# Second attention of a four-layer gated model: turned value products, with divisors spread by TensorE

## Chip, cores and metric

One NeuronCore of a Trainium2 chip. The metric is device time of one execution in microseconds (us); lower is better. TensorE is called PE, VectorE DVE, ScalarE ACT, GpSimd POOL, as in the profile.

## The reference, cut to what matters

The model takes x (2 batches of 1024 rows, 256 wide) through four gated layers, each a cross attention and a feed-forward part. The change touches only the second layer's attention:

```python
def _L1_xattn_ref(query, key, value, attention_bias, Wq, Wk, Wv, Wo):   # 16 heads of 16
    q = proj(query, Wq, SQ); k = proj(key, Wk, SKV); v = proj(value, Wv, SKV)
    scores = jnp.einsum('bhqd,bhkd->bhqk', q, k) / np.sqrt(HEAD_DIM)
    scores = scores + attention_bias[:, None, None, :]
    probs = jax.nn.softmax(scores, axis=-1)
    out = jnp.einsum('bhqk,bhkd->bhqd', probs, v)
    out = out.transpose(0, 2, 1, 3).reshape(B, SQ, EMBED)
    return out @ Wo.T
...
x = x + jnp.tanh(g_xattn[1]) * _L1_xattn_ref(_layernorm(x), ctx_1024, ctx_1024, fside_BxS2_0, ...)
```

There are 64 keys for each batch, so one tile of 128 queries has 16 heads x 64 keys = 1024 scores in each row. Softmax keeps its maximum and its divisor for each query and head.

## The kernel before, in words

The program writes five instruction streams by hand, one for each engine, which meet at counting semaphores. Each engine takes its stream strictly in the written order: an instruction whose wait is not met holds everything behind it. The 2048 queries are 16 tiles (`NT`) of 128. All of the second attention is the functions `pe_xattn` (L680), `act_xattn` (L725), `dve_xattn` (L748) and `pool_xattn` (L773), called with L = 1. Each is a loop over rounds i, and in a round each engine works on tiles of different ages.

For tile t the work goes like this. PE makes the scores (two products of 512 columns, in the round i = t). DVE adds the bias (L766) and takes the maxima of the 16 heads (L768), also in round t. POOL subtracts the maxima (L782, round t). ACT takes the exponentials (L746, its round t+1). PE turns them with eight transposes (L696, round t+2), so that keys lie on partitions. ACT copies the first half out of PSUM (L734) and DVE the second (L757). PE multiplies them with the values (round t+3): the exponentials are the stationary operand and a block of `VP`, 32 value columns and two columns of ones, is the moving one, so that both the values and the sums of the exponentials come out with queries on partitions. DVE takes the reciprocals of the sums (L423) and multiplies (L427, `dve_normalise`). PE turns the 256 columns with two transposes (L437, `pe_tr_o`, round t+4), ACT copies them (L445, `act_tr_o`), PE multiplies with the output weights (`pe_w_o`, round t+5). DVE adds the gated result to x (L458, `dve_w_o`), takes its statistics for the next layer norm (L171, L172) and normalises the tile before (L187). POOL makes the reciprocal standard deviation (L176, L177, `pool_rstd`, POOL's round t+5), for which it waits for that tile's statistics.

All products here are in float32; the trace shows two instructions, each with its weight load, for one product of the program, and one for a transpose. All products have the line L166 of the helper `mm`.

The buffers that make engines wait for each other: scores have two pairs of PSUM banks, `SXA` (shifted scores) and `EXA` (exponentials) have two tiles each, the turned exponentials one bank for each half, `EV` two tiles. So the bias addition of tile i waits for the exponentials of tile i-2, and the products behind the transposes wait with them.

Two orders matter for the prediction. DVE's round i before the change starts with the older tile: output, statistics and norm of tile i-5, then the copy of tile i-2, then bias and maxima of tile i, then `dve_normalise` of tile i-3. POOL's round i is `pool_rstd` of tile i-5, which waits for `s_bn` (statistics), and then the subtraction of tile i:

```python
def pool_xattn(e, L):
    for i in range(NT + 5):
        t = i - 5
        if 0 <= t < NT:
            pool_rstd(e, 16 * (2 * L + 1) + t + 1, t)
        t = i
        if t < NT:
            ...
            e.tensor_tensor(sv, sv, bc(MX[:, t % 2, :], 2, 64), ALU.subtract).then_inc(s_sb, 1)
```

Of the kernel before, what the change touches and what calls it, by code (L numbers as in the profile page):

```python
# [7 lines left out]
ACT = mybir.ActivationFunctionType  # L8
# [8 lines left out]
NT = 16  # L17
# [75 lines left out]
def build(nc, d, out):  # L93
    with ExitStack() as ctx:
# [191 lines left out]
        SMS = [[view(oR + 7520 + 64 * b + 8 * i, 8) for i in range(3)] for b in range(2)]  # L286
        RC = view(oR + 7544, 2, 16)
        ON = view(oXT, 2, 256)
        OT = view(oXT + 512, 2, 2, 128)
        RST8 = view(oR + 7944, 64)  # L290
        ETS = [view(oR + 8192, 8, 1024), view(oW + 8192, 8, 1024)]
# [89 lines left out]
        def pool_heads(e, L):  # L381
            if L == 0:
                settle(e, pool, e.memset(RST8, 1.0))
                settle(e, pool, e.memset(RST8.rearrange("p (e t) -> p e t", e=8)[:, :, 0], 0.0))
                e.memset(VP0, 0.0).then_inc(s_vz, 1)
                e.memset(view(NS0, 576), 0.0).then_inc(s_vz, 1)
                return
            settle(e, pool, e.memset(VP, 0.0))
            for h in range(2):
                e.memset(VP[64 * h:64 * h + 64, :, :, 32 + h:33 + h], 1.0).then_inc(s_vz, 1)  # L390

# [24 lines left out]
                        m = e.tensor_copy(ov, iv)  # L416
            m.then_inc(s_vp, 1)

        def dve_normalise(e, L, t, bank):
            pv = psum[:, bank, 0:272].rearrange("p (q n) -> p q n", q=8)  # L420
            rc = RC[:, t % 2, :].rearrange("p (q h) -> p q h", h=2)
            e.wait_ge(s_pv, PVB[L] + t + 1)
            settle(e, dve, e.reciprocal(rc, pv[:, :, 32:34]))  # L423
            ov = ON[:, t % 2, :].rearrange("p (q h c) -> p q h c", q=8, h=2)
            if L < 2 and t >= 2:
                e.wait_ge(s_to, t - 1)
            e.tensor_tensor(ov, pv[:, :, 0:32].rearrange("p q (h c) -> p q h c", h=2), bc(rc, 3, 16),  # L427
                            ALU.mult).then_inc(s_on, 1)

        def pe_tr_o(e, L, t):  # L430
            pt = psum[:, 7, 0:256].rearrange("p (k q) -> p k q", k=2)
            e.wait_ge(s_on, ONB[L] + t + 1)
            if t:
                e.wait_ge(s_ot, t)
                e.wait_ge(s_x, 32 * L + t)
            for k in range(2):
                m = e.transpose(pt[:, k, :], ON[:, t % 2, 128 * k:128 * k + 128], ident)  # L437
            m.then_inc(s_to, 1)

        def act_tr_o(e, L, t):  # L440
            pt = psum[:, 7, 0:256].rearrange("p (k q) -> p k q", k=2)
            e.wait_ge(s_to, t + 1)
            if t >= 2:
                e.wait_ge(s_wo, 16 * L + t - 1)
            e.activation(OT[:, t % 2, :, :], pt, ACT.Copy).then_inc(s_ot, 1)  # L445

        def pe_w_o(e, L, t, bank):
            Wt = weights(L)
            e.wait_ge(s_ot, t + 1)
            if t:  # L450
                e.wait_ge(s_x, 32 * L + t)
            for k in range(2):
                m = mm(e, psum[:, bank, 0:256], OT[:, t % 2, k, :], Wt[:, 3, k, :], k == 0, k == 1)
            m.then_inc(s_wo, 1)

        def dve_w_o(e, L, t, bank):
            e.wait_ge(s_wo, 16 * L + t + 1)
            e.scalar_tensor_tensor(out=xs(t), in0=psum[:, bank, 0:256], scalar=TG[:, L:L + 1], in1=xs(t),  # L458
                                   op0=ALU.mult, op1=ALU.add).then_inc(s_x, 1)
            dve_next_norm(e, 2 * L + 1, t)  # L460

# [218 lines left out]
        def pe_xattn(e, L):  # L680
            pe_heads(e, L)
            B = 16 * L
            for i in range(NT + 5):
                if L == 1 and 0 <= i - 5:
                    pe_w_o(e, L, i - 5, 7)
                t = i - 2
                if 0 <= t < NT:
                    e.wait_ge(s_ex, B + t + 1)
                    if t == 0:
                        e.wait_ge(s_q, 8 * L + 8)  # L690
                    for h in range(2):
                        pt = psum[:, 4 + h, :].rearrange("p (q n) -> p q n", q=4)
                        if t:
                            e.wait_ge(s_ea if h == 0 else s_ed, 16 * (L - 1) + t)
                        for q in range(4):
                            m = e.transpose(pt[:, q, :], EXA[:, t % 2, 128 * (4 * h + q):128 * (4 * h + q) + 128], ident)  # L696
                        m.then_inc(s_te, 1)
                t = i
                if t < NT:
                    bk = 2 * (t % 2)  # L700
                    e.wait_ge(s_q, 8 * L + 2 * (t // 4) + (4 if t == 1 else 2))
                    if t >= 2:
                        e.wait_ge(s_mx, 16 * L + t - 1)
# [5 lines left out]
                t = i - 4  # L709
                if L == 1 and 0 <= t < NT:  # L710
                    pe_tr_o(e, L, t)
                t = i - 3
                if 0 <= t < NT:
                    e.wait_ge(s_ea, 16 * (L - 1) + t + 1)
                    e.wait_ge(s_ed, 16 * (L - 1) + t + 1)
                    e.wait_ge(s_on, ONB[L] + t) if t else e.wait_ge(s_xt, 8 * RT[L] + 8)
                    for q in range(8):
                        m = mm(e, psum[:, 6, 34 * q:34 * q + 34], EV[:, t % 2, q, :], VP[:, t // 8, q, :], True, True)
                    m.then_inc(s_pv, 1)

        def act_table(e, func):

# [2 lines left out]
        def act_xattn(e, L):  # L725
            act_table(e, ACT.Exp)
            act_heads(e, L)
            for i in range(NT + 4):
                t = i - 2
                if 0 <= t < NT:  # L730
                    e.wait_ge(s_te, 32 * (L - 1) + 2 * t + 1)
                    if t >= 2:
                        e.wait_ge(s_pv, PVB[L] + t - 1)
                    e.activation(EV[:, t % 2, 0:4, :], psum[:, 4, :].rearrange("p (q n) -> p q n", q=4),  # L734
                                 ACT.Copy).then_inc(s_ea, 1)
                t = i - 4
                if L == 1 and 0 <= t < NT:
                    act_tr_o(e, L, t)
                if i < 2:
                    act_queries(e, L, i + 2)  # L740
                t = i - 1
                if 0 <= t < NT:
                    e.wait_ge(s_sb, 16 * (L - 1) + t + 1)
                    if t >= 2:
                        e.wait_ge(s_te, 32 * (L - 1) + 2 * t - 2)
                    e.activation(EXA[:, t % 2, :], SXA[:, t % 2, :], ACT.Exp).then_inc(s_ex, 1)  # L746

        def dve_xattn(e, L):  # L748
            for i in range(NT + 5):
                if 0 <= i - 5:  # L750
                    dve_w_o(e, L, i - 5, 7)
                t = i - 2
                if 0 <= t < NT:
                    e.wait_ge(s_te, 32 * (L - 1) + 2 * t + 2)
                    if t >= 2:
                        e.wait_ge(s_pv, PVB[L] + t - 1)
# [12 lines left out]
                t = i - 3  # L769
                if 0 <= t < NT:  # L770
# [2522 lines left out]
```

## Time and profile before

| what | value |
|---|---|
| runs of the kernel before, us | 1825.71, 1826.85, 1837.81 (median 1826.85) |
| the profiled execution's own time | 1830.78 us |
| its span in the profile | 1828.4 us |
| mean granted clock of PE | 0.942 of full speed |
| PE busy over the span | 90% |
| DVE, ACT, POOL busy | 60%, 50%, 45% |

The profiled execution is one run; its span leaves out 2.4 us of its own time, and its own time is 3.9 us over the median of the three. Every group of rows below is from this execution. A time stamp is in us from the start of the span. A busy time is that of an engine alone; a low share is no spare time if the engine stands at a wait that another engine ends.

### The profile page before, as it was taken

To read this page: it belongs to the slowest core of one execution; us is meant where nothing else is said; L and a number is where in the kernel's file an instruction comes from. 1 tells how busy PE (TensorE), PEld (TensorE's weight loads), DVE (VectorE), ACT (ScalarE), POOL (GpSimd) and SP (SyncE) were. 2 spreads that over 40 slices of the span, in tenths; PEclk is the share of its full clock that TensorE was granted. 3 is DMA by queue.
4 is the path that set the end of the run, shared out by engine and by line. 5 is a ranking of instruction groups with operands and counts; after the bars stand their busy time and mean duration, and the time that the engine had idled before them with its cause. 6 is when DMAs were issued, how large, how long until landed. Compare 5 with 4: busy or idle time off the path is not lost.

```text
span 1828.4 us, 26547 instructions
## 1 busy us (share of the span) xinstructions
PE 1646.0 (90%) x9339; PEld 1120.1 (61%) x9339; DVE 1103.6 (60%) x2244; ACT 915.9 (50%) x1534; POOL 816.8 (45%) x778
## 2 busy tenths in 40 slices
PE   6979999969977998889997987999999999987997
PEld 3469999837744333369983665555555655563774
DVE  5775676578784554544436997565666565554335
ACT  3324565323358997725544664655554456421463
POOL 3056112224373554430005563666675676835106
PEclk9779999989897999979998997999999999988999
DMA  9713333020000000252112000000000000022454
GB/s 352 264 50 99 126 141 132 29 108 1 15 9 1 4 8 5 87 236 73 48 55 89 1 1 35 1 1 1 1 1 1 1 1 1 1 92 74 135 156 138
DMA packets 61593, 117.51 MB, mean 64 GB/s; under 512 B 7215, under 2 KB 50211, under 8 KB 58776
## 3 DMA queue, kind: packets, MB, share of 16 engines
q1 hardware_dynamic: 53400, 95.64, 15.0%
q0 software_dynamic: 8064, 20.19, 3.4%
q8 instruction: 77, 1.26, 0.3%
q14 instruction: 52, 0.43, 0.1%
HBM read 71.99 MB, written 44.89 MB: 64 GB/s over the span
## 4 chain that ended last, share of the span: by engine, by line
PE 71%; DVE 14%; POOL 4%; issue 3%; ACT 3%; DMA 3%; SPq 0%; POOLq 0%; DVEq 0%; ACTq 0%
PE psum L166 66%; DMA arena<-xb 2%; POOL arena L884 2%; DVE arena L1847 1%; DVE arena L171 1%; PE psum L206 1%; POOL arena L1994 1%; DVE arena L187 1%; DVE arena L2548 1%; PE psum L696 1%; DVE arena L2109 1%; ACT arena L1723 1%; DVE rounded L2477 1%; DVE arena L1275 1%; PE psum L2417 1%
## 5 line engine op out<-in xcount | busy, mean ns | idle before, releaser
L166 PE MATMUL psum<-arena 128*128 128x128 f32 (+14 forms) x5276 | 1050.1, 434 | 88.8 <-DMA arena<-in_aw 12.5
L166 PEld LDWEIGHTS psum<-arena 128*128 128x128 f32 (+4 forms) x5276 | 603.5, 173 | 426.1 <-issue 282.6
L166 PE MATMUL psum<-rounded 128*128 128x270 f32 (+5 forms) x3008 | 528.8, 340 | 13.3 <-DVE arena L2548 4.4
L166 PEld LDWEIGHTS psum<-rounded 128*128 128x128 f32 (+2 forms) x3008 | 400.5, 190 | 150.0 <-issue 55.7
L2647 POOL TENSOR_TENSOR arena<-arena 128x1024 f32<-128x1024 f32 (+1 forms) x111 | 262.9, 2369 | 72.7 <-ACT arena L2597 65.4
L2548 DVE TENSOR_REDUCE arena<-psum 128x1 f32<-128x512 f32 x256 | 163.7, 682 | 101.3 <-PE psum L166 99.4
L2597 ACT ACTIVATE arena<-psum 128x1024 f32<-128x1024 f32 x144 | 145.0, 1023 | 98.0 <-PE psum L166 97.1
L1723 ACT ACTIVATE arena<-psum,arena 128x1024 f32<-128x1024 f32 x128 | 134.5, 1116 | 21.7 <-PE psum L166 20.2
L1304 POOL DMA_INDIRECT yt<-arena x40 | 40.2, 1004 | 147.7 <-DVE arena L1262 132.9
L939 DVE SCALAR_TENSOR_TENSOR rounded<-arena,rounded 128x540 fp32r<-128x540 f32 (+1 forms) x96 | 83.0, 886 | 24.6 <-ACT rounded L1184 22.4
L884 POOL DMA_INDIRECT arena<-yb,arena x48 | 46.3, 965 | 102.7 <-DMA yb<-arena 89.0
L1997 POOL TENSOR_TENSOR arena<-arena 128x256 f32<-128x256 f32 (+1 forms) x48 | 44.1, 931 | 92.7 <-ACT arena L1723 92.7
L176 POOL TENSOR_SCALAR arena<-arena 128x1 f32<-128x1 f32 x89 | 22.2, 249 | 139.1 <-DVE arena L172 118.3
L2477 DVE SCALAR_TENSOR_TENSOR rounded<-psum,rounded 64x512 fp32r<-64x512 f32 (+1 forms) x80 | 47.6, 595 | 43.7 <-ACT rounded L2440 22.6
L2644 POOL TENSOR_TENSOR arena<-arena 128x1024 f32<-128x1024 f32 x16 | 37.9, 2371 | 78.8 <-ACT arena L2597 78.8
L214 ACT ACTIVATE arena<-psum 128x512 f32<-128x512 f32 x48 | 27.8, 595 | 79.1 <-PE psum L206 78.6
L2619 DVE RECIPROCAL arena<-arena 128x128 f32<-128x128 f32 x64 | 58.9, 936 | 11.0 <-ACT arena L2464 10.5
L206 PE MATMUL psum<-arena 128*128 128x128 f32 x192 | 34.0, 318 | 30.7 <-DVE arena L187 29.1
L1176 ACT ACTIVATE arena<-psum,arena 128x28 f32<-128x28 f32 x64 | 17.9, 279 | 81.9 <-PE psum L166 81.9
L1941 DVE SCALAR_TENSOR_TENSOR arena<-psum,arena 128x128 f32<-128x128 f32 x92 | 26.1, 344 | 51.1 <-PE psum L166 51.0
L171 DVE BATCH_NORM_STATS2 arena<-arena 128x6 f32<-128x256 f32 x128 | 54.3, 424 | 3.3
L187 DVE TENSOR_SCALAR arena<-arena 128x256 f32<-128x256 f32 x128 | 50.5, 416 | 8.3 <-POOL arena L183 4.6
(278 smaller groups left out, 1942.5 us busy)
## 6 DMA issues: line engine op xcount, KB each, us to landing
arena<-in_w SPq DMA_DIRECT2D x8, 2048.0 KB, 8.0
yb<-arena SPq DMA_DIRECT2D x70, 128.0 KB, 1.7
arena<-xb SPq DMA_DIRECT2D x68, 128.0 KB, 2.2
arena<-in_w1u SPq DMA_DIRECT2D x4, 2048.0 KB, 13.8
xb<-arena SPq DMA_DIRECT2D x3, 2048.0 KB, 15.9
xb<-arena SPq DMA_DIRECT2D x2, 2064.0 KB, 32.6
arena<-xb SPq DMA_DIRECT2D x8, 516.0 KB
yt<-arena SPq DMA_DIRECT2D x2, 2048.0 KB, 16.3
```

The lines of the kernel that those rows point to most:

```text
L166: return e.matmul(o, l, r, start=start, stop=stop, skip_group_check=True)
L171: settle(e, dve, e.bn_stats(ST[:, t, :], src(t)))
L187: e.tensor_scalar(xn(t), src(t), MV[:, t, 0:1], RS[:, t:t + 1], ALU.subtract, ALU.mult).then_inc(s_xn, 1)
L206: m = e.transpose(pt[:, t, k, :], src(2 * i + t)[:, 128 * k:128 * k + 128], ident)
L884: e.indirect_dma_start(dst, None, buf, bass.IndirectOffsetOnAxis(idx[:, col:col + 1], 0)).then_inc(s_gth[s], 16)
L939: e.scalar_tensor_tensor(out=dst, in0=src, scalar=1.0, in1=hi, op0=ALU.mult, op1=ALU.subtract).then_inc(sig, 1)
L1723: e.activation(PT[:, u % 3, 2 * h:2 * h + 2, :], psum[:, bk:bk + 2, :], ACT.Exp, bias=NBD[:, 0:1]).then_inc(s_ae, 1)
L2477: e.scalar_tensor_tensor(out=lo, in0=psum[r, bk, 0:64 if (kind, c) == ("k", 2) else 512], scalar=1.0, in1=hi, op0=ALU.mult, op1=ALU.subtra ...
L2548: m = e.tensor_reduce(x3_MX[:, t, a, c:c + 1], psum[:, bk, :], AX.X, ALU.max)
L2597: e.activation(x3_P[0:rows, g % 4].rearrange("p a n -> p (a n)"), psum[0:rows, bk:bk + 2, :].rearrange("p a n -> p (a n)"), ACT.Exp, scale ...
L2619: e.reciprocal(x3_RC[:, 128 * i:128 * i + 128], x3_SM[:, 128 * i:128 * i + 128]).then_inc(s_rc3, 1)
L2647: m = e.tensor_tensor(ac, ac, x3_P[0:rows, g % 4], ALU.add)
```

## The change

The products of exponentials and values are turned round. `VP` becomes the stationary operand, with its 32 value columns, and a block of `EV` (128 queries) the moving one. Eight such products fill two squares of PSUM bank 6 with the values already turned (features on partitions); each writes one of four strips of 32 partitions. Eight more products with a matrix of ones and zeros (`ONES1`) give the sums. ACT copies values and sums together (`RAW`). PE turns the sums with one transpose, DVE takes 16 reciprocals for each query, ACT widens each to 16 columns (`RCB`), PE turns the widened divisors with two products against the identity, and DVE multiplies values and divisors straight into `OT`, from which the product with the output weights is made as before. ACT now copies both halves of the turned exponentials. The transposes of `pe_tr_o`, the copy of `act_tr_o` and DVE's copy are gone. POOL writes `ONES1` once, with three fills, in `pool_heads`.

The engines' rounds change too: the output of a tile is one round later on PE and DVE (`NT + 6` rounds), and in DVE's round bias and maxima now come first. `pool_xattn` is not in the diff. Cut to its core:

```diff
+        RAW = view(oXT + 1024, 3, 384)
+        ONES1 = view(oR + 6688, 68)
+        RCB = view(oXT + 2176, 2, 256)
...
+        def cross_kept1(t):
+            return t + 1 + max(0, t - 1)
...
+        def pe_cross_value1(e, t):
+            e.wait_ge(s_ea, t + 1)
+            e.wait_ge(s_ed, t + 1)
+            e.wait_ge(s_ot, cross_kept1(t - 1)) if t else e.wait_ge(s_xt, 8 * RT[1] + 8)
+            for q in range(8):
+                k, j = q // 4, q % 4
+                mm(e, psum[32 * j:32 * j + 32, 6, 128 * k:128 * k + 128], VP[:, t // 8, q, 0:32], EV[:, t % 2, q, :], True, True)
+            for q in range(8):
+                k, j = q // 4, q % 4
+                m = mm(e, psum[32 * j:32 * j + 32, 6, 256:384], ONES1[:, 32 * k:32 * k + 32], EV[:, t % 2, q, :], k == 0, k == 1)
+            m.then_inc(s_pv, 1)
+
+        def act_cross_value1(e, t):
...
+            e.activation(RAW[:, t % 3, :], psum[:, 6, 0:384], ACT.Copy).then_inc(s_ot, 1)
+
+        def pe_cross_turn_sums1(e, t):
...
+            e.transpose(psum[:, 6, 384:512], RAW[:, t % 3, 256:384], ident).then_inc(s_to, 1)
+
+        def dve_cross_divisors1(e, t):
+            e.wait_ge(s_to, t + 1)
+            if t + 1 < NT:
+                e.wait_ge(s_pv, PVB[1] + t + 2)
+            e.reciprocal(RC[:, t % 2, :].rearrange("p (a j h) -> p j a h", a=2, j=4), cross_sums1()).then_inc(s_rb, 1)
+
+        def act_cross_widen1(e, t):
...
+            e.activation(RCB[:, t % 2, :].rearrange("p (a c) -> p a c", c=16), bc(RC[:, t % 2, :], 2, 16),
+                         ACT.Copy).then_inc(s_ot, 1)
+
+        def pe_cross_spread1(e, t):
...
+            for k in range(2):
+                m = mm(e, psum[:, 7, 128 * k:128 * k + 128], RCB[:, t % 2, 128 * k:128 * k + 128], ident, True, True)
+            m.then_inc(s_vs, 1)
+
+        def dve_cross_value1(e, t):
+            e.wait_ge(s_vs, 4 + t + 1)
+            e.tensor_tensor(OT[:, t % 2].rearrange("p k n -> p (k n)"), RAW[:, t % 3, 0:256], psum[:, 7, 0:256],
                             ALU.mult).then_inc(s_on, 1)
...
         def pe_xattn(e, L):
-            for i in range(NT + 5):
-                if L == 1 and 0 <= i - 5:
-                    pe_w_o(e, L, i - 5, 7)
+            for i in range(NT + 6):
...
+                if 0 <= i - 6:
+                    pe_cross_w_o1(e, i - 6)
+                if 0 <= i - 5 < NT:
+                    pe_cross_spread1(e, i - 5)
+                if 0 <= i - 4 < NT:
+                    pe_cross_turn_sums1(e, i - 4)
+                if 0 <= i - 3 < NT:
+                    pe_cross_value1(e, i - 3)
...
         def dve_xattn(e, L):
-            for i in range(NT + 5):
-                if 0 <= i - 5:
-                    dve_w_o(e, L, i - 5, 7)
-                t = i - 2
-                if 0 <= t < NT:
...
-                    e.tensor_copy(EV[:, t % 2, 4:8, :], psum[:, 5, :].rearrange("p (q n) -> p q n", q=4)).then_inc(s_ed, 1)
+            for i in range(NT + 6):
                 t = i
                 if t < NT:
...
-                    dve_normalise(e, L, t, 6)
+                if 0 <= i - 5 < NT:
+                    dve_cross_value1(e, i - 5)
+                if 0 <= i - 6:
+                    dve_w_o(e, L, i - 6, 7, 256)
+                if 0 <= i - 4 < NT:
+                    dve_cross_divisors1(e, i - 4)
```

How the rows now stand. DVE, one round in the middle of the second attention before the change; L766 is the bias addition, L768 the maxima, L172 the statistics that POOL waits for:

```order
L458 SCALAR_TENSOR_TENSOR arena<-psum,arena 128x256 [waits o_prod]
L171 BN_STATS arena<-arena 128x6 [waits x_tile]
L172 BN_AGGR arena<-arena 128x2 [waits dve]
L187 TENSOR_SCALAR arena<-arena 128x256 [waits rstd]
L757 COPY arena<-psum 128x512 [waits values,e_turned]
L766 TENSOR_TENSOR arena<-psum,arena 128x1024 [waits exps,scores]
L768 TENSOR_REDUCE arena<-arena 128x16 [waits dve]
L423 RECIPROCAL arena<-psum 128x16 [waits values]
L427 TENSOR_TENSOR arena<-psum,arena 128x256 [waits o_turned,dve]
```

DVE, one round at the same place after the change; L798 and L800 are the bias addition and the maxima, L485 the product with the divisors, L499 the output:

```order
L798 TENSOR_TENSOR arena<-psum,arena 128x1024 [waits exps,scores]
L800 TENSOR_REDUCE arena<-arena 128x16 [waits dve]
L485 TENSOR_TENSOR arena<-arena,psum 128x256 [waits v_scaled]
L499 SCALAR_TENSOR_TENSOR arena<-psum,arena 128x256 [waits o_prod]
L171 BN_STATS arena<-arena 128x6 [waits x_tile]
L172 BN_AGGR arena<-arena 128x2 [waits dve]
L187 TENSOR_SCALAR arena<-arena 128x256 [waits rstd]
L466 RECIPROCAL arena<-psum 128x4x2x2 [waits values,o_turned]
```

The statistics stood ahead of a round's bias and maxima, for tile i-5; they now stand behind them, for tile i-6.

POOL in the changed kernel, from the first five subtractions (L817) on; the rows of before are the same with L782:

```order
L817 TENSOR_TENSOR arena<-arena 128x1024 [waits maxima] x5
L176 TENSOR_SCALAR arena<-arena 128x1 [waits bn_stats]
L177 TENSOR_TENSOR arena<-arena 128x1 [waits pool]
L817 TENSOR_TENSOR arena<-arena 128x1024 [waits maxima]
L176 TENSOR_SCALAR arena<-arena 128x1 [waits bn_stats]
L177 TENSOR_TENSOR arena<-arena 128x1 [waits pool]
```

Nothing moved here: the subtraction of tile 5 stands behind the statistics of tile 0, that of tile 6 behind those of tile 1, and so on.

PE, one round in the middle after the change; L735 turns exponentials, 512 columns are scores, 256 the output product, L460 turns the sums, 32x128 are values and sums:

```order
L735 MATMUL psum<-arena 128x128 [waits e_kept_a,exps]
L735 MATMUL psum<-arena 128x128 x3
L735 MATMUL psum<-arena 128x128 [waits e_kept_d]
L735 MATMUL psum<-arena 128x128 x3
L166 MATMUL psum<-arena 128x512 [waits maxima,q_ready]
L166 MATMUL psum<-arena 128x512
L166 MATMUL psum<-arena 128x256 [waits x_tile,o_normed]
L166 MATMUL psum<-arena 128x256
L166 MATMUL psum<-arena 128x128 [waits o_normed,o_kept]
L166 MATMUL psum<-arena 128x128
L460 MATMUL psum<-arena 128x128 [waits divisors_spread,o_kept]
L166 MATMUL psum<-arena 32x128 [waits o_kept,e_kept_d,e_kept_a]
L166 MATMUL psum<-arena 32x128 x15
```

The transposes and scores still open the round, and the output product has moved behind them.

## Rows read from the trace of the kernel before

**Rows 1.** Stretch; us; busy of PE, PEld, DVE, ACT, POOL; granted clock; DMA share, GB/s.

```profile
440.00:460.00 20.00, 20.00 (x133) 16.38 (x132) 18.72 (x33) 7.45 (x12) 8.99 (x10) 1.00 0.00 1
```

**Rows 2.** Chain that ended last, one round: start us, us, what.

```profile
442.80 0.87 PE psum L696 x8
443.67 1.72 PE psum L166 x4
445.61 2.65 PE psum L166 x20
```

**Rows 3.** Timeline, one round of DVE and POOL: start us, us, what, idle before.

```profile
442.64 0.43 DVE L427 TENSOR_TENSOR arena<-psum,arena 128x256 f32<-128x256 f32 x1
442.98 0.48 DVE L458 SCALAR_TENSOR_TENSOR arena<-psum,arena 128x256 f32<-128x256 f32 x1
...
443.49 0.43 DVE L171 BATCH_NORM_STATS2 arena<-arena 128x6 f32<-128x256 f32 x1
...
443.95 0.18 DVE L172 BATCH_NORM_AGGREGATE arena<-arena 128x2 f32<-128x6 f32 x1
...
444.51 0.19 POOL L176 TENSOR_SCALAR arena<-arena 128x1 f32<-128x1 f32 x1
444.78 0.54 POOL L177 TENSOR_TENSOR arena<-arena 128x1 f32<-128x1 f32 x1
```

**Rows 4.** Timeline of the stage's first rounds, from tile 2's subtraction on.

```profile
412.21 1.90 POOL L782 TENSOR_TENSOR arena<-arena 128x1024 f32<-128x1024 f32 x1 [7.17 <-DVE arena L768]
...
414.15 1.06 ACT L746 ACTIVATE arena<-arena 128x1024 f32<-128x1024 f32 x1 [3.46 <-POOL arena L782]
...
415.26 1.09 PE L696 MATMUL psum<-arena 128*128 128x128 f32 x8 [1.34 <-ACT arena L746]
...
416.19 1.88 PE L166 MATMUL psum<-arena 128*128 128x512 f32 x4
...
418.11 1.22 DVE L766 TENSOR_TENSOR arena<-psum,arena 128x1024 f32<-128x1024 f32 x1 [1.03 <-PE psum L166]
...
419.37 1.22 DVE L768 TENSOR_REDUCE arena<-arena 128x16 f32<-128x1024 f32 x1
...
424.07 1.05 ACT L746 ACTIVATE arena<-arena 128x1024 f32<-128x1024 f32 x1
```

**Rows 5.** Timeline of the stage's end: last exponentials, an output product, last output.

```profile
482.70 1.06 ACT L746 ACTIVATE arena<-arena 128x1024 f32<-128x1024 f32 x1
...
496.84 2.07 PE L166 MATMUL psum<-arena 128*128 128x256 f32 x4 [0.47 <-ACT arena L445]
...
498.95 0.48 DVE L458 SCALAR_TENSOR_TENSOR arena<-psum,arena 128x256 f32<-128x256 f32 x1 [2.41 <-PE psum L166]
```

**Rows 6.** Groups of this stage: shape xcount | busy us, mean ns | idle before.

```profile
L166 PE MATMUL psum<-arena 128*128 128x34 f32 x256 | 31.5, 280 | 0.0
```

**Rows 7.** The same view, 600 to 800 us: products with 32 stationary columns.

```profile
L166 PE MATMUL psum<-arena 128*32 128x128 f32 x120 | 6.2, 272 | 0.0
```

**Rows 8.** PE at half clock: timeline, then the chain.

```profile
377.51 6.70 PE L166 MATMUL psum<-arena 128*128 128x512 f32 x8 [0.69 <-ACT arena L214]
...
499.50 3.79 PE psum L206 x16
```

**Rows 9.** Stretches round a gap of PE, columns as in Rows 1.

```profile
1108.00:1110.00 2.00, 0.00 (x0) 0.00 (x0) 1.87 (x6) 1.93 (x4) 1.43 (x3) 1.00 0.00 0
1111.00:1113.00 2.00, 2.00 (x9) 1.80 (x9) 1.27 (x4) 1.40 (x3) 0.74 (x2) 0.50 0.04 8
1114.00:1116.00 2.00, 2.00 (x20) 1.98 (x19) 0.51 (x2) 0.60 (x1) 0.00 (x0) 0.99 0.02 4
```

**Rows 10.** The gap's end in the timeline, and POOL's idle time after its fills.

```profile
1110.70 0.39 PE L2258 MATMUL psum<-arena 128*128 128x128 bf16 x2 [2.92 <-ACT arena L2307]
...
369.69 0.33 POOL L182 TENSOR_SCALAR arena<-arena 128x2 f32<-128x2 f32 x1 [6.46 <-DVE arena L172]
```

More of the change, by code:

```diff
@@ L388, in pool_heads @@
             settle(e, pool, e.memset(VP, 0.0))
+            if L == 1:
+                settle(e, pool, e.memset(ONES1, 0.0))
+                for h in range(2):
+                    settle(e, pool, e.memset(ONES1.rearrange("p (a x) -> p a x", a=2)[:, :, 0:32].rearrange(
+                        "p a (r f) -> p a r f", f=4)[64 * h:64 * h + 64, :, :, h], 1.0))
             for h in range(2):
@@ L417, in dve_heads, with cross_sums1 @@
             m.then_inc(s_vp, 1)
[L419 to L427, printed above, removed]
+        def cross_sums1():
+            return psum[:, 6, 384:512].rearrange("p (j x) -> p j x", j=4)[:, :, 0:4].rearrange("p j (a h) -> p j a h", a=2)
@@ new lines, in cross_kept1, with cross_widened1 @@
+        def cross_kept1(t):
+            return t + 1 + max(0, t - 1)
+        def cross_widened1(t):
+            return min(t + 2, NT) + t + 1
+        def pe_cross_value1(e, t):
[9 more added lines that the diff above has]
+            m.then_inc(s_pv, 1)
@@ new lines, in act_cross_value1 @@
+        def act_cross_value1(e, t):
+            e.wait_ge(s_pv, PVB[1] + t + 1)
+            if t:
+                e.wait_ge(s_rb, 8 + t)
+            if t >= 3:
+                e.wait_ge(s_on, ONB[1] + t - 2)
+            e.activation(RAW[:, t % 3, :], psum[:, 6, 0:384], ACT.Copy).then_inc(s_ot, 1)
+        def pe_cross_turn_sums1(e, t):
+            e.wait_ge(s_ot, cross_kept1(t))
+            if t:
+                e.wait_ge(s_rb, 8 + t)
+            e.transpose(psum[:, 6, 384:512], RAW[:, t % 3, 256:384], ident).then_inc(s_to, 1)
@@ new lines, in dve_cross_divisors1 @@
+        def dve_cross_divisors1(e, t):
[4 more added lines that the diff above has]
+        def act_cross_widen1(e, t):
+            e.wait_ge(s_rb, 8 + t + 1)
+            if t >= 2:
+                e.wait_ge(s_vs, 4 + t - 1)
+            e.activation(RCB[:, t % 2, :].rearrange("p (a c) -> p a c", c=16), bc(RC[:, t % 2, :], 2, 16),
+                         ACT.Copy).then_inc(s_ot, 1)
@@ new lines, in pe_cross_spread1 @@
+        def pe_cross_spread1(e, t):
+            e.wait_ge(s_ot, cross_widened1(t))
+            if t:
+                e.wait_ge(s_on, ONB[1] + t)
+            for k in range(2):
[4 more added lines that the diff above has]
+            e.tensor_tensor(OT[:, t % 2].rearrange("p k n -> p (k n)"), RAW[:, t % 3, 0:256], psum[:, 7, 0:256],
@@ L428, in dve_normalise, with pe_cross_w_o1 @@
                             ALU.mult).then_inc(s_on, 1)
-        def pe_tr_o(e, L, t):
-            pt = psum[:, 7, 0:256].rearrange("p (k q) -> p k q", k=2)
-            e.wait_ge(s_on, ONB[L] + t + 1)
+        def pe_cross_w_o1(e, t):
+            Wt = weights(1)
+            e.wait_ge(s_on, ONB[1] + t + 1)
             if t:
-                e.wait_ge(s_ot, t)
-                e.wait_ge(s_x, 32 * L + t)
+                e.wait_ge(s_x, 32 + t)
             for k in range(2):
-                m = e.transpose(pt[:, k, :], ON[:, t % 2, 128 * k:128 * k + 128], ident)
-            m.then_inc(s_to, 1)
@@ L440, in act_tr_o @@
[L440 to L453, printed above, removed]
+                m = mm(e, psum[:, 7, 256:512], OT[:, t % 2, k, :], Wt[:, 3, k, :], k == 0, k == 1)
@@ L454, in pe_w_o, with dve_w_o @@
             m.then_inc(s_wo, 1)
-        def dve_w_o(e, L, t, bank):
+        def dve_w_o(e, L, t, bank, at=0):
             e.wait_ge(s_wo, 16 * L + t + 1)
-            e.scalar_tensor_tensor(out=xs(t), in0=psum[:, bank, 0:256], scalar=TG[:, L:L + 1], in1=xs(t),
+            e.scalar_tensor_tensor(out=xs(t), in0=psum[:, bank, at:at + 256], scalar=TG[:, L:L + 1], in1=xs(t),
                                    op0=ALU.mult, op1=ALU.add).then_inc(s_x, 1)
@@ L708, in pe_xattn @@
                         pe_queries(e, L, t + 2)
[L709 to L712, printed above, removed]
-                if 0 <= t < NT:
[L714 to L719, printed above, removed]
+                if 0 <= i - 6:
[6 more added lines that the diff above has]
+                    pe_cross_value1(e, i - 3)
         def act_table(e, func):
@@ L735, in act_xattn @@
                                  ACT.Copy).then_inc(s_ea, 1)
-                t = i - 4
-                if L == 1 and 0 <= t < NT:
-                    act_tr_o(e, L, t)
+                    e.wait_ge(s_te, 32 * (L - 1) + 2 * t + 2)
+                    e.activation(EV[:, t % 2, 4:8, :], psum[:, 5, :].rearrange("p (q n) -> p q n", q=4),
+                                 ACT.Copy).then_inc(s_ed, 1)
                 if i < 2:
@@ L746, in act_xattn @@
                     e.activation(EXA[:, t % 2, :], SXA[:, t % 2, :], ACT.Exp).then_inc(s_ex, 1)
+                if 0 <= i - 3 < NT:
+                    act_cross_value1(e, i - 3)
+                if 0 <= i - 4 < NT:
+                    act_cross_widen1(e, i - 4)
         def dve_xattn(e, L):
-            for i in range(NT + 5):
-                if 0 <= i - 5:
-                    dve_w_o(e, L, i - 5, 7)
-                t = i - 2
[L753 to L756, printed above, removed]
-                    e.tensor_copy(EV[:, t % 2, 4:8, :], psum[:, 5, :].rearrange("p (q n) -> p q n", q=4)).then_inc(s_ed, 1)
+            for i in range(NT + 6):
                 t = i
@@ L768, in dve_xattn @@
                     e.tensor_reduce(MX[:, t % 2, :], sv, AX.X, ALU.max).then_inc(s_mx, 1)
-                t = i - 3
-                if 0 <= t < NT:
-                    dve_normalise(e, L, t, 6)
+                if 0 <= i - 5 < NT:
+                    dve_cross_value1(e, i - 5)
+                if 0 <= i - 6:
+                    dve_w_o(e, L, i - 6, 7, 256)
+                if 0 <= i - 4 < NT:
+                    dve_cross_divisors1(e, i - 4)
         def pool_xattn(e, L):
```

## The prediction

> **What bounds the kernel now.** I read the busy times of the stage first, then the chain that ended last, then the timeline of one round on the engines that hand work to each other. In the middle of the second attention PE is busy for all 20 us of a stretch, at full granted clock; DVE is busy for 18.7, ACT for 7.5, POOL for 9.0 [rows 1]. The chain runs through PE alone, and one round is 0.87 (eight transposes) + 1.72 (scores) + 2.65 (values and the output product) and the two transposes of `pe_tr_o`, 0.22 at the same 0.109 each: 5.46 us a tile [rows 2]. So PE's work sets the pace.
>
> A second view matters more here: who waits for whom in a circle. Tile 2's way is subtraction at 412.21, exponentials 414.15, transposes 415.26, the next scores 416.19, their bias 418.11, their maxima 419.37 [rows 4]. These scores belong to a tile two further on, so the circle closes once in two tiles and leaves PE the bound. It stays so only because POOL's wait for statistics ahead of a subtraction is met early: DVE takes the statistics of tile i-5 in front of the bias of tile i, and POOL does L176 and L177 [rows 3] while it would wait for the maxima anyway.
>
> **The change on PE.** Removed for each tile: 16 value instructions of 34 columns, 31.5 / 256 = 0.123 us each [rows 6], 1.97 us, and the two transposes, 0.22. Added: 32 instructions with 32 stationary columns and 128 moving ones. The same shape elsewhere takes 6.2 / 120 = 0.052 us each [rows 7], so 1.66 us. If four ran entirely as one, they would take 32 / 4 x 0.107 (a quarter of a 512-column instruction, 0.43 us [rows 2]) = 0.86; if none ran beside another, 3.4. I take 1.66, the row of the same shape. Added too: one transpose, 0.11, and four instructions of 128 columns for the spread, 0.43. PE's round is then 0.87 + 1.72 + 0.86 (output product, 4 x 0.215, half of a 512-column instruction) + 0.43 + 0.11 + 1.66 = 5.65 us, against 5.46. Taken alone the change is worth about nothing on PE: between -0.6 and +2 us a tile.
>
> **The other engines.** ACT gains a copy of 512 columns, one of 384 and one of 256, and loses one of 256. Each is shorter than its pass over 1024 columns, 1.06 us [rows 4]; with 7.45 us in 20 [rows 1], 2.0 a tile, it stays under 5.3 and is not the bound. DVE loses its copy. POOL's three extra fills come once, ahead of an idle stretch of 6.46 us [rows 10], so they cost nothing; a fill that outlasted it would delay the next stage's statistics by the same time.
>
> **The change in order, and the wait that it makes.** DVE now does bias and maxima of tile i first, then the product with the divisors of tile i-5, and the output and statistics of tile i-6. POOL's order is as it was: statistics of tile i-5, then the subtraction of tile i. The statistics of tile i-5 now come in DVE's round i+1, behind the maxima of tile i+1. So the subtraction of tile i waits until DVE has finished bias and maxima of the next tile. Behind it on POOL stand all later subtractions, and for its result waits the exponential of tile i. But the scores of tile i+1 stand on PE behind the transposes of tile i-1, and these wait for the exponentials of tile i-1. The circle thus closes once for every tile, without a deadlock, from tile 5 on.
>
> One turn at full clock, in order: exponentials to transposes 1.11, to scores 0.93, to bias 1.92, to maxima 1.26, the maxima 1.22 [rows 4]; the product to the output 0.34, to the statistics 0.51, to the aggregate 0.46, that 0.18; POOL's two instructions 0.27 + 0.54 [rows 3]; two handovers of 0.05 (the subtraction's end to the exponentials is 0.04); the subtraction up to the exponentials 1.94 [rows 4]. Sum 10.78, say 10.8 us. PE's other work of the round, 0.86 + 0.43 + 0.11 + 1.66 = 3.1, falls in the shadow of DVE and POOL; the spread is done before DVE has its maxima. So PE stands idle for 10.8 - 5.65 = 5.1 us in each turn.
>
> **What the clock makes of that.** After a gap of 2.92 us that ended at 1110.70 [rows 10] the next burst ran at 0.50 (1.2 GHz), though the clock had still been 1.00 in the gap; by 1114 it was back [rows 9], some 3.3 us into the burst. A gap of 5.1 us in every turn should do the same. The transposes then take 3.79 / 16 x 8 = 1.90 us [rows 8], 0.97 more than the 0.93. The scores take 6.70 / 8 = 0.84 each at half clock [rows 8]; 1.4 us of the 3.3 are left for them, 1.7 of four instructions, the other 2.3 at 0.43: 2.4 us, 0.7 more. A turn is 10.8 + 1.0 + 0.7 = 12.5. If the clock stayed at 1.00 it is 10.8; if it returned only after the scores, 10.8 + 0.97 + 4 x 0.41 = 13.4. I take 12.5, as rows 9 have such a gap.
>
> The Trainium skill, "TensorE: Matmul & The Clock Gate", section "Why this matters for your kernels", advises against idle gaps between bursts of products, because the engine falls back to half clock. By that rule every turn starts slow and the sum is the one with 12.5; without it, the one with 10.8, some 17 us less. The trace agrees at rows 9.
>
> **The sum.** Before, the exponentials of tile 4 start at 424.07 [rows 4] and those of tile 15 at 482.70 [rows 5]: 58.6 us. After: the first turn from tile 4 to 5 has had no gap yet, 10.8; nine turns from tile 5 to tile 14 at 12.5 are 112.5; the last turn has no scores, bias and maxima any more and instead waits for PE's output product and spread: 1.11 + 1.90 + 1.6 (four instructions take 2.07 at half clock [rows 5], a part is past the return) + 0.5 + 0.05 + 0.34 + 0.51 + 0.46 + 0.18 + 0.05 + 0.81 + 0.05 + 1.94 = 9.5. Together 132.8, so +74.2.
>
> The rounds before tile 5 are lighter on PE, as only two or three of the four new steps run; I take -1.5 (0 to -3). The end was 498.95 + 0.48 - 482.70 = 16.7 us from the last exponentials to the last output, at half clock for its most part [rows 5]. After, it is a chain with more handovers (values, copy, transposed sums, reciprocals, widening, spread, product, output) but without the stall of two transposes behind each output: I take no change, -3 to +3. The rest of the program is the same code, only later. In all +73 us. Against the profiled execution's own 1830.78 that is 1903.8; it lies 3.9 over the median of the runs shown, so I predict 1826.85 + 73 = 1900.
>
> **The rivals.** First, the same circle at another clock: all turns at 10.8 with a last one of 7.8 (9.5 less 0.97 and 0.7) make 115.8, +57, less 1.5: 1882; all at 13.4 with a last of 10.4 (output product and spread wholly at half clock) make 144.4, +86, less 1.5: 1911. With the bounds of beginning and end these reach from 1878 to 1916.
>
> Second, on the other side: POOL's wait is met in time and the circle stays one of two tiles. Then PE decides again, at 4.9 to 5.65 us a tile against 5.46; over 13 rounds -8 to +3, so 1819 to 1830, not slower. It decides from the point at which statistics of tile i-5 are there before the maxima of tile i. Rows 3 show that they were so before; the new order of DVE speaks against it, since it puts them a whole round later while POOL's rows are unmoved.
>
> "TensorEngine Tiling (Array Packing)", section "Key Properties", of the Trainium skill says that going from whole-array products to narrow strips, and back, drains TensorE. In this rival two such changes a round would add to PE; in the circle they lie in its idle time, and the 0.052 of rows 7 was measured in a stretch that mixes both, so the trace has no large price for it.
>
> Third, the narrow products don't run side by side: 32 x 0.107 = 3.4 us, PE's round 7.4. In the circle that still fits in 12.5 and costs only at the end, some 2 us; without the circle it would be 13 x 1.9 = +25, so 1852. Rows 7 speak against it.
>
> **How the numbers follow.** The forecast, the circle with a slow start in every turn: 0.62. The same circle at full clock throughout: 0.16; at half clock through the scores: 0.13. POOL's wait met in time: 0.06, of which 0.02 is left to a gain of over 1%, should PE's steps come cheaper still than their bounds. The third rival without the circle: 0.03. About 1% (18 us) is what a measurement of this kernel can tell from no change. So slower 0.94, within 1% 0.04, faster 0.02. The range takes in both clocks of the circle with the bounds of beginning and end, 1876 to 1918.
>
> **What would show it.** Right: in the changed profile L817 on POOL starts once in some 12.5 us from tile 5 on, with idle time before L176 that ends at DVE's L172; PE is busy for about half of the stage's middle with a granted clock between 0.6 and 0.9; transposes L735 wait for the exponentials for about 5 us each; the stage's steady part is about 133 us instead of 59. The step on the narrow products is right if they take some 1.7 us a round at full clock. Wrong: if L817 starts every 5 to 6 us, the circle is not there; if turns take 10.8 at a clock of 1.00, the part on the clock falls; if most of the loss lies after the last exponentials, my end is wrong.

## The result and the profile after

The changed kernel takes 1905.34 us in the median of four runs, against 1827.16 for the kernel before measured beside it. One of the four runs, 2169.64 us at a granted clock of 0.725, was in a slower state and is left out of the ratio, which is 1.0414 with a 95% interval of 1.0383 to 1.0445. The other three have a median of 1904.6, so the change costs some 77 us; 1900 was forecast, with a range of 1876 to 1918. The profiled execution took 1904.6 us with a span of 1902.8, 74.4 more than the span before, whose execution was 3.9 us over its own median.

The timeline of the changed kernel over two subtractions of POOL in turn, POOL's rows alone (start us, us, what, idle before and what ended it):

```profile
443.62 0.26 POOL L176 TENSOR_SCALAR arena<-arena 128x1 f32<-128x1 f32 x1 [9.76 <-DVE arena L172]
443.96 0.56 POOL L177 TENSOR_TENSOR arena<-arena 128x1 f32<-128x1 f32 x1
444.48 1.91 POOL L817 TENSOR_TENSOR arena<-arena 128x1024 f32<-128x1024 f32 x1
456.70 0.26 POOL L176 TENSOR_SCALAR arena<-arena 128x1 f32<-128x1 f32 x1 [10.31 <-DVE arena L172]
457.04 0.54 POOL L177 TENSOR_TENSOR arena<-arena 128x1 f32<-128x1 f32 x1
457.54 1.90 POOL L817 TENSOR_TENSOR arena<-arena 128x1024 f32<-128x1024 f32 x1
```

These answer to [rows 3]. Before, L176 ran at once, in the time in which POOL waited for the next maxima, as the subtraction that followed it there shows:

```profile
447.98 1.90 POOL L782 TENSOR_TENSOR arena<-arena 128x1024 f32<-128x1024 f32 x1 [2.66 <-DVE arena L768]
```

Now POOL stands ten us at L176 itself, what ends that is DVE's L172, and the subtraction follows at once. One turn here is 457.54 - 444.48 = 13.06 us.

What stands between, on PE and on DVE, in the same timeline:

```profile
447.53 1.97 PE L735 MATMUL psum<-arena 128*128 128x128 f32 x8 [5.50 <-ACT arena L782]
449.29 4.71 PE L166 MATMUL psum<-arena 128*128 128x512 f32 x12
453.84 0.27 PE L460 MATMUL psum<-arena 128*128 128x128 f32 x1
454.04 1.08 PE L166 MATMUL psum<-arena 128*32 128x128 f32 x32
...
452.73 1.23 DVE L798 TENSOR_TENSOR arena<-psum,arena 128x1024 f32<-128x1024 f32 x1 [8.74 <-PE psum L166]
453.99 1.22 DVE L800 TENSOR_REDUCE arena<-arena 128x16 f32<-128x1024 f32 x1
455.13 0.41 DVE L485 TENSOR_TENSOR arena<-arena,psum 128x256 f32<-128x256 f32 x1
455.45 0.48 DVE L499 SCALAR_TENSOR_TENSOR arena<-psum,arena 128x256 f32<-128x256 f32 x1
455.97 0.43 DVE L171 BATCH_NORM_STATS2 arena<-arena 128x6 f32<-128x256 f32 x1
456.43 0.18 DVE L172 BATCH_NORM_AGGREGATE arena<-arena 128x2 f32<-128x6 f32 x1
```

Read it as a circle: exponentials (446.42, 1.06 long) release the transposes at 447.53, the scores behind them release the bias at 452.73, then maxima, product, output and statistics follow one another, and the statistics' end at 456.61 releases POOL at 456.70. PE had been idle for 5.50 us when the transposes began, and it took 1.97 us for them where [rows 4] have 1.09; from their start to the scores it was 1.76 where [rows 4] have 0.93.

The groups of the whole stage, 395 to 582 us (count | busy us, mean ns | idle just before, and what ended it):

```profile
L735 PE MATMUL psum<-arena 128*128 128x128 f32 x128 | 26.8, 377 | 61.9 <-ACT arena L782 61.9
L798 DVE TENSOR_TENSOR arena<-psum,arena 128x1024 f32<-128x1024 f32 x16 | 19.6, 1224 | 90.9 <-PE psum L166 90.9
L782 ACT ACTIVATE arena<-arena 128x1024 f32<-128x1024 f32 x16 | 16.9, 1056 | 98.2 <-POOL arena L817 98.2
L176 POOL TENSOR_SCALAR arena<-arena 128x1 f32<-128x1 f32 x16 | 4.0, 253 | 122.2 <-DVE arena L172 122.2
```

All four engines now wait, each for the next one of the circle. PE's transposes wait 61.9 us for ACT, ACT 98.2 for POOL, POOL 122.2 for DVE, and DVE 90.9 for PE. No engine is a bound; a circle of waits shows as this ring of idle times. A stretch of 40 us (busy us of PE, PEld, DVE, ACT, POOL, then the granted clock) answers to [rows 1]:

```profile
440.00:480.00 40.00, 23.64 (x162) 15.92 (x161) 13.08 (x25) 8.80 (x15) 8.02 (x9) 0.74 0.00 1
```

PE is busy for 59% at a clock of 0.74, where it was busy throughout at 1.00.

### The profile page after: what moved, and what is told of

It reads as the page before. It is cut to its first block, busy times and chain, and to the rows that moved or that the text cites. A ratio compares the mean times of both kernels' runs of the same rounds, so it can differ in the third digit from the quotient of the medians.

```text
span 1902.8 us, 27191 instructions
## 1 busy us (share of the span) xinstructions
PE 1656.0 (87%) x9643; PEld 1116.4 (59%) x9643; DVE 1090.8 (57%) x2228; ACT 930.1 (49%) x1566; POOL 817.7 (43%) x781
## 4 chain that ended last, share of the span: by engine, by line
PE 47%; DVE 11%; POOL 4%; ACT 3%; issue 3%; DMA 2%; SPq 0%; POOLq 0%; DVEq 0%; ACTq 0%
PE psum L166 44%; DMA arena<-xb 2%; POOL arena L919 2%; DVE arena L1882 1%; POOL arena L2029 1%; DVE arena L171 1%; DVE arena L2583 1%; DVE arena L2144 1%; ACT arena L1758 1%; DVE rounded L2512 1%; DVE arena L187 1%; PE psum L206 1%; PE psum L2452 1%; DVE arena L2173 0%; DVE arena L1870 0%
## 5 line engine op out<-in xcount | busy, mean ns | idle before, releaser
L166 PE MATMUL psum<-arena 128*128 128x128 f32 (+15 forms) x5596 | 1053.4, 425 | 90.9 <-DMA arena<-in_aw 12.2
L176 POOL TENSOR_SCALAR arena<-arena 128x1 f32<-128x1 f32 x89 | 22.9, 257 | 244.4 <-DVE arena L172 224.4
L735 PE MATMUL psum<-arena 128*128 128x128 f32 x128 | 26.8, 377 | 61.9 <-ACT arena L782 61.9
L798 DVE TENSOR_TENSOR arena<-psum,arena 128x1024 f32<-128x1024 f32 x16 | 19.6, 1224 | 90.9 <-PE psum L166 90.9
L782 ACT ACTIVATE arena<-arena 128x1024 f32<-128x1024 f32 x16 | 16.9, 1056 | 98.2 <-POOL arena L817 98.2
L735 PEld LDWEIGHTS psum<-arena 128*128 128x128 f32 x128 | 21.2, 195 | 67.1 <-ACT arena L782 66.9
L206 PE MATMUL psum<-arena 128*128 128x128 f32 x192 | 32.0, 305 | 32.1 <-DVE arena L187 29.8
```

Of the source, the lines that this page charges most:

```text
L166: return e.matmul(o, l, r, start=start, stop=stop, skip_group_check=True)
L206: m = e.transpose(pt[:, t, k, :], src(2 * i + t)[:, 128 * k:128 * k + 128], ident)
```

## The experiments

The theory on trial: POOL's wait for statistics, which the change moved to a later round of DVE while POOL's order stayed, closes the circle once for every tile (the step in "The change in order"). Rival A: the new chain from values to output, with more handovers, sets the round by itself. A second question was what the clock adds.

**POOL one round later (e1).** The edit to the changed kernel:

```diff
-            for i in range(NT + 5):
-                t = i - 5
+            for i in range(NT + 6):
+                t = i - 6
                 if 0 <= t < NT:
                     pool_rstd(e, 16 * (2 * L + 1) + t + 1, t)
```

> The changed kernel with one edit: POOL makes the reciprocal deviation of tile i-6, not i-5, ahead of the subtraction of tile i (22 rounds). Theory (the circle through POOL's wait for statistics): the wait is now met in DVE's own round, so the circle closes once in two tiles again, 8.46 us (transposes at 406.80 and 415.26 in the kernel before) + 0.42 + 0.51 + 0.46 + 0.18 + 0.05 + 0.81 for the product, the output, the statistics and POOL's two instructions, which still stand between maxima and subtraction: 10.9 for two tiles, 5.4 a tile, so the time is that of the kernel before, 1822 to 1832. Rival A (the longer chain of new steps, copy, turned sums, reciprocals, widening, spread, sets the round, not POOL's wait): it stays at about 1905.

Measured: 1826.42 us, ratio to the kernel before 1.0008, interval 0.9994 to 1.0023. POOL's rows:

```profile
445.46 0.26 POOL L176 TENSOR_SCALAR arena<-arena 128x1 f32<-128x1 f32 x1 [2.52 <-DVE arena L172]
...
446.31 1.91 POOL L817 TENSOR_TENSOR arena<-arena 128x1024 f32<-128x1024 f32 x1
...
451.74 1.90 POOL L817 TENSOR_TENSOR arena<-arena 128x1024 f32<-128x1024 f32 x1
```

POOL still waits for DVE's L172, but 2.5 us, and the round shown is 5.43. The whole loss is gone with every new step of the value chain in place, so rival A is out. The statistics still stand between maxima and subtraction here, as the expectation said.

**POOL two rounds later (e2).** The same edit with 7 in place of 6.

> The changed kernel with POOL making the reciprocal deviation of tile i-7 ahead of the subtraction of tile i (23 rounds). Theory: these statistics are a round old, nothing stands between maxima and subtraction, and PE sets the pace with 0.87 + 1.72 + 0.86 + 0.43 + 0.11 + 1.08 (the 32 narrow products as measured after the change) = 5.1 us a tile against 5.46 before: 12 x 0.36, about 4 us faster than the kernel before, 1818 to 1826, and faster than lag 6 by 1 to 5 us. Rival A (the new steps set the round): about 1905.

Measured: 1827.24 us, ratio 1.0001, interval 0.9986 to 1.0015. Two subtractions on POOL, and one round of PE:

```profile
445.30 1.91 POOL L817 TENSOR_TENSOR arena<-arena 128x1024 f32<-128x1024 f32 x1 [2.50 <-DVE arena L800]
447.29 0.19 POOL L176 TENSOR_SCALAR arena<-arena 128x1 f32<-128x1 f32 x1
...
450.48 1.90 POOL L817 TENSOR_TENSOR arena<-arena 128x1024 f32<-128x1024 f32 x1 [2.37 <-DVE arena L800]
```

```profile
444.05 1.08 PE L166 MATMUL psum<-arena 128*32 128x128 f32 x32
445.07 1.09 PE L735 MATMUL psum<-arena 128*128 128x128 f32 x8
446.00 3.19 PE L166 MATMUL psum<-arena 128*128 128x512 f32 x12
449.02 0.27 PE L460 MATMUL psum<-arena 128*128 128x128 f32 x1
449.23 1.08 PE L166 MATMUL psum<-arena 128*32 128x128 f32 x32
```

The mechanism came out: L176 no longer waits, the subtraction waits for the maxima, and the round shown, 449.23 - 444.05 = 5.18 us, is PE's own work. The expected gain on the total, 4 us, did not show, nor one over e1: the interval allows from -2.6 to +2.7 us. The stage alone is shorter by about that much: from the first exponentials to the last output it takes 90.6 us (406.24 to 496.85), 91.8 in e1 (404.72 to 496.55) and 93.3 in the kernel before (405.70 to 498.95), each in one execution. Neither e1 nor e2 beats the kernel before by more than the measurement can tell.

**The kernel before with POOL's order alone moved (e4).** No new product; the statistics are asked for two rounds early:

```diff
-            for i in range(NT + 5):
-                t = i - 5
+            for i in range(NT + 3):
+                t = i - 3
```

> The kernel before the change with POOL's order alone moved: the reciprocal deviation of tile i-3 ahead of the subtraction of tile i (19 rounds), no new product. Theory: the statistics of tile i-3 come in DVE's round i+2, behind PE's rounds i+1 and the output product of i+2, which wait for the exponentials of tile i-1; a circle for every tile of 1.11 + 0.93 + 1.88 + 0.22 + 1.97 + 0.87 + 0.51 + 0.46 + 0.18 + 0.05 + 0.81 + 0.05 + 1.94 = 11.0 us at full clock, 12.7 to 13.4 with bursts that start at half clock, from tile 3 on: 11 turns at 7.2 to 7.9 us more than 5.46 and a shorter last one, 1905 to 1930. Rival A (only the new value steps make the loss): 1827.

Measured in a single run: 1934.84 us, against 1825.88 beside it. The first and the last exponentials of eleven turns, and POOL's wait:

```profile
424.69 1.06 ACT L746 ACTIVATE arena<-arena 128x1024 f32<-128x1024 f32 x1 [6.38 <-POOL arena L782]
574.07 1.06 ACT L746 ACTIVATE arena<-arena 128x1024 f32<-128x1024 f32 x1 [6.32 <-POOL arena L782]
```

```profile
448.84 0.26 POOL L176 TENSOR_SCALAR arena<-arena 128x1 f32<-128x1 f32 x1 [10.76 <-DVE arena L172]
```

A turn is (574.07 - 424.69) / 11 = 13.58 us. The wait alone, put into the old kernel, makes a loss of the same kind, with the same ten us at L176. It is larger, 109 us against 77, as the circle opens two tiles earlier and a turn is longer. The time lies 5 us above the expected 1905 to 1930. A turn was 0.2 us longer than the upper bound of 13.4, which over eleven turns is 2 us, and the turn into tile 3, ahead of these eleven, had already grown from 4.46 us in the kernel before to 10.94 (413.75 to 424.69).

**PE's gap filled (e3).** Behind the narrow products PE gets four products in rounds 5 to 14 that nobody reads:

```diff
+                if 5 <= i < NT - 1:
+                    e.wait_ge(s_mx, 16 * L + i)
+                    for k in range(4):
+                        mm(e, psum[:, 2 * ((i + 1) % 2) + k % 2, :], qT[:, 0, 128 * i:128 * i + 128], KB[:, 0, 0, :], True, True)
```

> The changed kernel with work added on PE alone: in rounds 5 to 14, behind the narrow products, four score products (eight instructions of 512 columns, 3.4 us at full clock) whose results are overwritten unread. Theory on the clock (the gap of some 5.5 us makes every burst start at half clock): the gap shrinks to about 2 us, the clock stays at 1.00, a turn falls from 13.0 to 10.8 us, nine to ten turns: 18 to 22 us faster than the changed kernel, about 1885. Rival B (the clock is not what makes a turn 13.0 and not 10.8; the extra work is hidden): 1905. Rival C (the extra work stands in the way): up to 10 x 3.4 more, 1939.

Measured: 1889.59 us, ratio to the kernel before 1.0344, interval 1.0321 to 1.0367, so some 15 us less than the changed kernel's 1904.6. The stretch, PE's rows and the exponentials of nine turns:

```profile
440.00:480.00 40.00, 34.45 (x242) 20.32 (x241) 16.96 (x32) 9.78 (x18) 9.38 (x12) 1.00 0.00 1
```

```profile
450.33 1.09 PE L735 MATMUL psum<-arena 128*128 128x128 f32 x8 [1.87 <-ACT arena L786]
451.26 3.19 PE L166 MATMUL psum<-arena 128*128 128x512 f32 x12
...
454.49 4.71 PE L166 MATMUL psum<-arena 128*32 128x128 f32 x40
461.03 1.09 PE L735 MATMUL psum<-arena 128*128 128x128 f32 x8 [1.83 <-ACT arena L786]
```

```profile
438.48 1.06 ACT L786 ACTIVATE arena<-arena 128x1024 f32<-128x1024 f32 x1 [7.76 <-POOL arena L821]
534.89 1.06 ACT L786 ACTIVATE arena<-arena 128x1024 f32<-128x1024 f32 x1 [7.83 <-POOL arena L821]
```

With 1.85 us of idle time left the clock stays at 1.00, and a turn is (534.89 - 438.48) / 9 = 10.71 us, the 10.8 of the prediction's sum at full clock. So the clock's share of a turn is 2.3 us. The total gained a little less than the expected 18 to 22: the filling of round 5 came before the circle had opened, and the turn from tile 4 to 5 took 13.87 us (424.61 to 438.48) where it is 10.65 without.

**Half the filling (e7).** Two products instead of four, rounds 6 to 14.

> The changed kernel with half of the filling work: in rounds 6 to 14, two score products (1.7 us at full clock) behind the narrow products, overwritten unread. Theory on the clock: PE's gap is then some 3.7 us where a turn is at full clock; in the kernel before one gap of 3.71 us (up to 554.95) let the clock fall and one of 2.26 us (up to 726.10) did not, so most turns should still start at half clock and take 12.5 to 13.3: 1895 to 1906. Rival: the smaller gap already keeps the clock, turns of 10.7, 1883 to 1887.

Measured: 1900.24 us, ratio 1.0397, interval 1.0328 to 1.0466. PE's gap, and the clock in it and in the burst after it:

```profile
456.53 1.97 PE L735 MATMUL psum<-arena 128*128 128x128 f32 x8 [3.15 <-ACT arena L786]
```

```profile
454.00:456.00 2.00, 0.00 (x0) 0.00 (x0) 0.00 (x0) 0.57 (x1) 1.39 (x1) 1.00 0.00 0
457.00:459.00 2.00, 2.00 (x9) 1.64 (x8) 0.00 (x0) 1.22 (x3) 0.00 (x0) 0.50 0.02 4
```

```profile
431.01 1.06 ACT L786 ACTIVATE arena<-arena 128x1024 f32<-128x1024 f32 x1 [6.44 <-POOL arena L821]
544.18 1.06 ACT L786 ACTIVATE arena<-arena 128x1024 f32<-128x1024 f32 x1 [9.57 <-POOL arena L821]
```

The clock fell at the end of this gap of 3.15 us, and a turn is (544.18 - 431.01) / 9 = 12.57 us. It was not so in every turn. In three of the nine, after gaps of 3.55 to 3.58 us, the transposes still ran at full clock (1.09 us) and the clock fell during the burst: at 445.9, where the burst had begun at 444.54. So the length of the gap alone doesn't say when the clock falls. As a whole e7 can't be told from the changed kernel, as their intervals overlap. Gaps between e3's 1.85 us and 3.15 were not tried in this stage.

**DVE's round reordered (e5).** POOL as in the change; on DVE the output and statistics stand first again:

```diff
             for i in range(NT + 6):
+                if 0 <= i - 6:
+                    e.wait_ge(s_vs, 4 + min(i - 5, NT - 1) + 1)
+                    dve_w_o(e, L, i - 6, 7, 256)
                 t = i
...
                     dve_cross_value1(e, i - 5)
-                if 0 <= i - 6:
-                    dve_w_o(e, L, i - 6, 7, 256)
```

> The changed kernel with DVE's round reordered: the output, statistics and norm of tile i-6 stand first in the round again (behind a wait for the spread of tile i-5), then bias and maxima of tile i, then the product with the divisors and the reciprocals. POOL as in the change (lag 5). Theory: the circle still closes for every tile, as the statistics of tile i-5 come in DVE's round i+1, but bias and maxima of tile i+1 are no longer in it: 1.11 + 0.93 + 1.72 + 0.86 + 0.43 + 0.05 + 0.51 + 0.46 + 0.18 + 0.05 + 0.81 + 0.05 + 1.94 = 9.1 us at full clock, against 10.7; PE's gap is some 4 us, so bursts start at half clock as a rule and a turn is about 10.8 to 11.3: 1860 to 1890. Rival D (it is the position of the statistics in DVE's round that matters, not the round): 1827. Rival A (the new value steps set the round): 1905.

Measured: 1891.77 us, ratio 1.035, interval 1.0281 to 1.0419. The exponentials of nine turns, and POOL:

```profile
429.67 1.06 ACT L782 ACTIVATE arena<-arena 128x1024 f32<-128x1024 f32 x1 [5.04 <-POOL arena L818]
532.94 1.06 ACT L782 ACTIVATE arena<-arena 128x1024 f32<-128x1024 f32 x1 [8.56 <-POOL arena L818]
```

```profile
449.55 0.26 POOL L176 TENSOR_SCALAR arena<-arena 128x1 f32<-128x1 f32 x1 [8.21 <-DVE arena L172]
```

A turn is (532.94 - 429.67) / 9 = 11.47 us. The circle is still there, shorter by 12.98 - 11.47 = 1.5 us. So it is the round in which the statistics come that closes it, and what stands ahead of them in that round sets its length. I had expected 10.8 to 11.3 for a turn and 1860 to 1890 in all: in this circle the output product and the spread lie on the path too and ran partly at half clock, which that sum had not counted. In the turn from 452.33 to 464.64 the three together took 5.40 us up to the output, where the sum has 1.72 + 0.86 + 0.43 = 3.01:

```profile
455.20 5.36 PE L166 MATMUL psum<-arena 128*128 128x512 f32 x12
460.60 0.48 DVE L499 SCALAR_TENSOR_TENSOR arena<-psum,arena 128x256 f32<-128x256 f32 x1 [7.95 <-PE psum L166]
```

## Why the prediction was right

**The wait.** "The subtraction of tile i waits until DVE has finished bias and maxima of the next tile" is what the rows show, and e1, e2 and e4 show that this wait alone makes the loss and that taking it away takes all of it away. The second rival (POOL's wait met in time, about no change) turned out to be the true price of the rest of the change: e1 and e2 lie within 0.3% of the kernel before.

**A turn.** Forecast 12.5 us; the nine turns between the subtractions at 431.96 and 548.78 take 12.98 each. At full clock the sum was 10.8, and e3 measured 10.71. The mis-sized term is the return of the clock. I took 3.3 us into a burst, as at [rows 9], so that half of the scores would run at full clock. In the turn shown above (stretch, us, busy of PE, PEld, DVE, ACT and POOL, granted clock):

```profile
445.00:446.00 1.00, 0.00 (x0) 0.00 (x0) 0.00 (x0) 0.00 (x0) 1.00 (x1) 0.76 0.00 0
448.00:450.00 2.00, 2.00 (x9) 1.63 (x8) 0.00 (x0) 1.22 (x3) 0.00 (x0) 0.50 0.00 0
453.00:455.00 2.00, 2.00 (x40) 1.63 (x38) 1.97 (x2) 0.00 (x0) 0.00 (x0) 1.00 0.03 8
```

the clock falls within the gap, and the scores run from 449.29 to the bias at 452.73, 3.44 us, practically all at half clock (four times 0.84 of [rows 8] is 3.36). The Trainium skill's advice against gaps between bursts ("TensorE: Matmul & The Clock Gate", section "Why this matters for your kernels") held in all of these turns, and e3 is its counterproof. Each of the nine bursts began at half clock, its transposes took 1.97 us. Turns vary from 12.0 to 13.3, between the bounds 10.8 and 13.4 that were given, and they follow the clock's return: 12.03 us where it came 2.8 us into the burst, 12.53 at 3.7, 12.83 at 4.4, 13.05 at 4.8, and 13.25 to 13.29 in the five turns where it came at 5.2 us or later, when the scores were done or nearly so. So 12.5 is about right for a return at 3.3 us; the return came later than that in eight turns of nine.

**The sum.** The steady part from the exponentials of tile 4 (423.24) to those of tile 15 (560.03) took 136.8 us where 132.8 was forecast; nine turns at 0.48 more make up the difference. The first turn took 10.65 (10.8 forecast), the last 9.32 (9.5). The beginning, from the first exponentials to those of tile 4, took 16.9 us (406.35 to 423.24) where it was 18.4 before (405.70 to 424.07): the forecast's -1.5. The end, 577.84 + 0.48 - 560.03 = 18.3 us, is 1.6 longer than before, where no change was forecast, inside the +-3.

```profile
423.24 1.06 ACT L782 ACTIVATE arena<-arena 128x1024 f32<-128x1024 f32 x1
560.03 1.06 ACT L782 ACTIVATE arena<-arena 128x1024 f32<-128x1024 f32 x1 [5.60 <-POOL arena L817]
577.84 0.48 DVE L499 SCALAR_TENSOR_TENSOR arena<-psum,arena 128x256 f32<-128x256 f32 x1 [0.31 <-PE psum L166]
```

Added up, the stage from its first exponentials to its last output grew from 93.3 us to 171.5, by 78.2 where the forecast had 73; the medians grew by 77. The spans of the two profiled executions grew by 74.4 only, as what follows the stage took 1329.5 us in the one of before and 1324.9 in the one of after. That code is the same in every run, and in the profiles of the six experiments it took 1326.1 to 1330.8 us, so these 4.5 us are about what one execution differs from another. "The rest of the program is the same code, only later" stands. The forecast was 5 us short, and the clock's return in the nine turns (4.3 us) and the longer end (1.6) make that up. One sum of the first rival is off: 144.4 counts the first turn at 13.4 as well, though no gap stands before it; with 10.8 it is 141.8, and that rival's 1911 is about 1909, which moves neither the forecast nor the range.

**The narrow products.** Forecast 1.66 us for 32, measured 1.08 at full clock (0.034 each), nearer to the bound of 0.86 than to the row I took. The misreading is the mean of [rows 7]: its 120 instructions are 15 groups of eight, 0.41 us a group. From eight to 32 instructions is 0.67 us more, 0.028 each, about a quarter of the 0.107 of a whole-array instruction of 128 columns. So four ran as one, and each group bears some 0.2 us beside, which the eight transposes show as well (1.09 us where eight times 0.107 is 0.86). Divided by eight, these 0.2 us looked like a price of each instruction. The error cost nothing here, as these products lie in PE's idle time. It matters without the circle: PE's round became 5.18 us in e2, against 5.65 as forecast and 5.46 before. The third rival (the products don't run side by side) is excluded by the same rows: that would have been 3.4 us.

## What to carry to other kernels

When one engine's stream is reordered, write down for each other engine in which round it asks for what moved, and follow the wait back to where it started. Here a wait that had been met in time became a circle when its producer came one round later than its consumer asked, and the cure was one number on an engine that the change did not touch. In the profile the sign was a ring: every engine idle, each waiting for the next. If PE idles between bursts, price the burst twice, once at each clock.

## What the runs showed of the hardware that was not expected

Adding 3.4 us of products that nobody reads to every turn made the kernel some 15 us faster (e3), as it left PE a gap of 1.85 us and the clock at 1.00 throughout; with half as much (e7, gaps of 3.15 to 3.58 us) the clock fell in the gap or in the burst behind it, and a turn was 12.57 us. The place in a burst at which the clock came back was not fixed: 3.3 us into it at [rows 9], some 4.8 us into that of the turn shown, which began at 447.53 (up to 452 the clock is 0.50, from 452 to 453 it is 0.83 in the mean), and 2.8 to 6.0 us into the nine bursts of the circle.
